# A two-layer block on one core: a new order ahead of a selective scan, the scan's slots in its second half, the tail by halves, and the causal mask of the maxima on VectorE

## The reference

```
mod = silu(c) @ wmod                      # per layer: shift, scale, gate for two branches
# layer 0, branch 1: a selective scan over the tokens, 512 channels, 16 states
h    = layernorm(x) * (1 + scale) + shift
dt_in, B, C = split(h @ x_proj_w.T)       # 16, 16, 16
dt   = softplus(dt_in @ dt_proj_w.T + dt_b)
s_t  = exp(dt_t * A) * s_(t-1) + dt_t * B_t * h_t ;  y_t = sum_n s_t[n] * C_t[n] + D * h_t
x    = x + g(gate) * y                    # g clamps the gate away from zero
# layer 0, branch 2: base linear layer + LoRA experts weighted by softmax routing
w    = top-8 of softmax(h @ router_W.T), summed by expert
x    = x + g(gate) * (h @ base_W.T + b + sum_e w_e (h A_e) B_e)
# layer 1, branch 1: attention, 32 heads of 16, ALiBi, causal
attn = softmax(where(k <= q, q.k / 16 + slope * (k - q), -inf)) ; x = x + g * (attn v @ w_proj + b)
# layer 1, branch 2: gated feed-forward, 1376 wide
```

## Time and profile before

| | |
|---|---|
| median of three runs | 991.18 us (986.23 to 992.69) |
| the profiled execution | 988.8 us, span 987.0 us |
| busy, share of the span | PE 89%, DVE 76%, ACT 45%, POOL 27% |
| mean granted TensorE clock | 0.957 of full |

### The profile page before, as it was taken

How to read it: one execution, slowest core, us unless ns; L and a number is a source line. 1 busy time by engine, 2 the same in 40 slices (tenths; PEclk the granted TensorE clock), 3 DMA queues, 4 the chain that set the end, 5 groups by cost and what they waited for, 6 DMA issues and landing times.

```text
span 987.0 us, 12212 instructions
## 1 busy us (share of the span) xinstructions
PE 877.2 (89%) x4378; PEld 423.7 (43%) x4384; DVE 749.6 (76%) x1191; ACT 439.2 (45%) x822; POOL 264.5 (27%) x213
## 2 busy tenths in 40 slices
PE   3678868887776899989999999999999999999996
PEld 3224424443224544434455555555444444444442
DVE  6579999888899565637887788787524699876776
ACT  1637575645552102110066666666752465533200
POOL 1027789887894300005000000000000144200000
PEclk8769899999997999997999999999999999999998
DMA  9100060300002202451022211220006000000001
GB/s 353 65 1 0 1 255 1 128 0 1 0 0 72 100 0 89 135 181 38 15 69 74 74 37 40 73 75 2 2 1 224 5 0 1 0 1 0 12 33 43
DMA packets 29382, 54.35 MB, mean 55 GB/s; under 512 B 8021, under 2 KB 14805, under 8 KB 28041
## 3 DMA queue, kind: packets, MB, share of 16 engines
q1 hardware_dynamic: 29320, 53.57, 16.2%
HBM read 44.96 MB, written 8.39 MB: 54 GB/s over the span
## 4 chain that ended last, share of the span: by engine, by line
PE 58%; DVE 5%; SPq 3%; issue 3%; ACT 1%; DMA 0%; POOL 0%; DVEq 0%; POOLq 0%
PE ps L1075 15%; PE ps L940 8%; PE ps L922 6%; PE ps L1086 6%; PE ps L904 4%; PE ps L909 3%; PE ps L996 3%; PE ps L976 3%; SPq L302 2%; PE ps L857 2%; PE ps L962 2%; PE ps L925 1%; PE ps L907 1%; PE ps L851 1%; PE ps L725 1%
## 5 line engine op out<-in xcount | busy, mean ns | idle before, releaser
L678 ACT ACTIVATE prob<-ps 128x512 f32<-128x512 f32 x288 | 161.8, 599 | 138.6 <-PE ps L925 105.9
L458 POOL TENSOR_TENSOR hC<-hs,C_sb 128x512 f32<-128x512 f32 x128 | 163.0, 1284 | 70.1 <-DVE hs L1240 59.5
L832 PE MATMUL ps<-hC,identf 128*128 128x512 f32 x256 | 137.1, 644 | 35.6 <-POOL hC L458 33.5
L1354 DVE TENSOR_REDUCE mrow<-ps 128x4 f32<-128x512 f32 x160 | 103.7, 687 | 24.1 <-PE ps L907 15.8
L922 PE MATMUL ps<-stack 123*128 123x512 bf16 (+3 forms) x384 | 113.7, 327 | 0.2
L414 POOL TENSOR_TENSOR rstd<-veps,mhalf 128x4 f32<-128x4 f32 x8 | 8.4, 1052 | 381.4 <-DVE veps L1113 381.4
L612 ACT ACTIVATE ps<-dtT,nA 128x512 f32<-128x512 f32 x128 | 88.3, 691 | 42.2 <-DVE hs L1240 42.0
L1357 DVE TENSOR_REDUCE mrow<-ps 128x1 f32<-128x512 f32 x128 | 82.2, 685 | 25.1 <-PE ps L909 25.1
L832 PEld LDWEIGHTS ps<-hC,identf 128*128 128x128 f32 x256 | 45.3, 197 | 109.5 <-POOL hC L458 90.9
L1218 DVE TENSOR_TENSOR dBx<-uT,ps 128x512 f32<-128x512 f32 x112 | 74.9, 669 | 21.0 <-ACT B_sb L590 14.4
L940 PE MATMUL ps<-prob,V 128*32 128x512 f32 (+3 forms) x768 | 81.6, 498 | 0.7 <-ACT prob L678 0.7
(11 more groups left out here) (192 smaller groups left out, 1328.0 us busy)
## 6 DMA issues: line engine op xcount, KB each, us to landing
stack<-parts_dram SPq DMA_DIRECT2D x192, 64.0 KB
wmod<-in_wmod SPq DMA_DIRECT2D x4, 1536.0 KB, 11.2
parts_dram<-qkp SPq DMA_DIRECT2D x48, 128.0 KB, 1.8
wmod<-in_wmod SPq DMA_DIRECT2D x4, 1024.0 KB, 9.9
wattn<-in_wattn SPq DMA_DIRECT2D x1, 3072.0 KB, 10.3
wg<-in_wg SPq DMA_DIRECT2D x1, 2752.0 KB, 12.2
wu<-in_wu SPq DMA_DIRECT2D x1, 2752.0 KB, 9.5
wd<-in_wd SPq DMA_DIRECT2D x1, 2560.0 KB, 11.5
```

The lines of the kernel that those rows point to most:

```text
L458: pool.tensor_tensor(hC[:, c, :], hs[:, c, :], C_sb[:, m % 2, :], ALU.mult).then_inc(S["hc_done"], 1)
L678: A_(prob[:, u % 4, j, :], ps[:, 3 + F % 3, :], ACT.Exp).then_inc(S["exp_done"], 1)
L832: mm(ps[:, c, :], identf[:], hC[:, c, :], start=False, stop=(s == NS - 1), skip_group_check=True).then_inc(S["sum_done"], 1)
L1354: v.reduce_max(mrow[:, kb, :, i], ps[:, bank, :].rearrange("p (j c) -> p j c", c=P), AX) \
```

## The change

Four places are edited.

- Ahead of the scan: the second half's transposes move behind the first half's split. B and C are split by ScalarE, which copies the negated value in bfloat16, while TensorE adds it to the bank to leave the rest; three such copies per half. The signs of `sel` are turned to match. VectorE takes over the Relu (`arguments`). Half 1's dt_in, split and two of its four `z_out` come ahead of step 0. `dgD` is made earlier.
- Slots: two half rows in place of each full row. In the second half (`m >= 16`) a slot stands ahead of the third sum of a step, once the *next* step's C has been copied out, and ScalarE reads it a step later. Half 1's softplus has four ScalarE operations a step and ends one step earlier on POOL.
- Crossing and tail: `turn(0, c)` and the copies at step 16 are gone. Steps 25 to 28 have slots that make x + gated y of one token tile in bank 4 (identity matmul and four turns), which ScalarE copies to `x_tok`. Behind the scan only half 1 is added. Norm, transposes and router go by halves, with base outputs between them; base_out(4) is made ahead of the LoRA outputs. SP's bias loads wait for `yt`, not `x0`.
- Maxima: the second matmul is gone. Once, TensorE makes the mask in bank 2 and VectorE copies it to `negT` (bfloat16). A diagonal unit is reduced by four `tensor_tensor_reduce`, one per head: add the mask, write the sum to PSUM, and the maximum to `mrow`.

```diff
-            return range(3 * (n - 1), min(3 * n, 7 * DC)) if 1 <= n < NS else range(0)
+            return range(4 * (n - 1), min(4 * n, 7 * DC)) if 1 <= n < NS else range(0)
...
+            SLOTS[1 + i_] = ("cols", 0, 2 + i_ // 2, i_ % 2 * 2)
+        for i_ in range(2):
+            SLOTS[7 + i_] = ("row", 0, 5, i_)
+        for i_, m_ in enumerate((12, 13, 14, 15, 17, 18, 19, 20)):
+            SLOTS[m_] = ("cols", 1, (0, 1, 3, 4)[i_ // 2], i_ % 2 * 2)
+        for i_ in range(4):
+            SLOTS[21 + i_] = ("row", 1, (2, 5)[i_ // 2], i_ % 2)
+            SLOTS[25 + i_] = ("y", None, None, i_)
...
# ScalarE
+            for part in range(3):
+                bc_part(0, part)
+            for c in range(DC - 1):
+                soft(c)
+            ln_out(0, 0, 0, 1, (1,))
+            soft(DC - 1)
...
+            A_(dtin[:], ps[0:RANK, 0, :], ACT.Copy).then_inc(S["xp_in"], 1)
+            bc_part(1, 0)
+            z_out(1)
+            bc_part(1, 1)
+            z_out(2)
+            bc_part(1, 2)
...
-                    if m == NS and c >= 2:
-                        for t in (2 * c - 4, 2 * c - 3):
-                            act.wait_ge(S["yt"], t + 1)
-                            A_(uT[:, t, half(0)], ps[:, t, :], ACT.Copy).then_inc(S["yb"], 1)
...
+                    if c == 2 and m > NS and m - 1 in SLOTS and m - 1 >= NS:
+                        slot_out(m - 1)
# TensorE
+            def bc_rest(h, part):
+                rows = slice(32 * part, 32 * part + 32)
+                pe.wait_ge(S["bc_part"], 2 * h + part + 1)
+                mm(ps[32:64, 0, :], identb[rows, rows], BCs[rows, half(h)], start=False, stop=True, skip_group_check=True) \
+                    .then_inc(S["bc_sub"], 1)
...
+            dt_proj(0, 0)
+            bc_rest(0, 0)
+            dt_proj(0, 1)
+            bc_rest(0, 1)
+            dt_proj(0, 2)
+            dt_proj(0, 3)
+            pe.wait_ge(S["xp_bc"], 1)
+            ln_transpose(0, 1)
             x_proj(1)
...
+                pe.wait_ge(S["c_evac"], m + 1 if m < NS else m + 2)
...
+                    mm(ps[:, C_BANK, :], identf[:], x_tok[:, part, :], start=True, stop=False, skip_group_check=True)
+                    for c in range(DC):
+                        ins = mm(ps[:, C_BANK, c * P:(c + 1) * P], dtT[:, c, tile(part)], dgA[:, c, :], start=False,
+                                 stop=(c == DC - 1), skip_group_check=True)
...
             broadcast(0)
+            pe.wait_ge(S["xp_in"], 2)
+            dt_proj(1, 1)
+            bc_rest(1, 0)
+            dt_proj(1, 2)
+            bc_rest(1, 1)
+            dt_proj(1, 3)
+            pe.wait_ge(S["xp_bc"], 2)
+            dt_proj(1, 0)
...
-                    if c == 0 and m in SLOTS:
-                        modulation(m)
+                    if c == 0 and m in SLOTS and m < NS or c == 2 and m in SLOTS and m >= NS:
+                        slot(m)
...
+            ln_transpose(1, 0)
+            pe.wait_ge(S["in_lf"], 48)
+            router(0)
+            ln_transpose(1, 1)
+            base_out(0)
+            router(1)
+            for t in range(1, 4):
                 base_out(t)
...
+            base_out(4)
             pe.wait_ge(S["hw_evac"], 2)
-            for t in range(4):
+            for t in range(5):
                 lora_out(t)
...
-                        if kb == i:
-                            ins = mm(ps[:, bank, tile(j_)], negm[:], identb[:], start=False, stop=True)
# VectorE
+            def arguments(c):
+                v.wait_ge(S["sp_a"], c + 1)
+                ts(dtT[:, c, half(0)], ps[:, 4 + c, :], dtb[:, c:c + 1], 0.0, ALU.add, ALU.max).then_inc(S["sp_rd"], 1)
...
             ln_var(0)
+            ln_norm(1, 0)
+            for t in range(4, NT):
+                v.wait_ge(S["yt"], t + 1)
+                tt(x_tok[:, t, :], x_tok[:, t, :], ps[:, t, :], ALU.add).then_inc(S["x0"], 1)
...
+                if kb == i:
+                    for j_ in range(GH):
+                        ins = v.tensor_tensor_reduce(ps[:, bank, tile(j_)], ps[:, bank, tile(j_)], negT[:], 1.0, LOW,
+                                                     ALU.add, ALU.max, mrow[:, kb, j_, i:i + 1])
+                    ins.then_inc(S["m_done"], 1)
```

More of the change, by code:

```diff
@@ L542, in _, with bc_part, soft @@
-            for b in range(DC):
-                soft(b)
-            soft_ln(DC - 1)
+            ln_out(0, 0, 0, 1, (0,))
+            def bc_part(h, part):
+                if part:
+                    act.wait_ge(S["bc_sub"], 2 * h + part)
+                else:
+                    act.wait_ge(S["xp_in"], h + 1)
+                A_(BCs[32 * part:32 * part + 32, half(h)], ps[32:64, 0, :], ACT.Copy, scale=-1.0) \
+                    .then_inc(S["xp_bc" if part == 2 else "bc_part"], 1)
+            def soft(c):
+                src = ps[:, 4 + c, :]
+                act.wait_ge(S["dt_mm"], c + 1)
+                A_(sp_log[:, c, :], src, ACT.Abs, bias=dtb[:, c:c + 1]).then_inc(S["sp_a"], 1)
+                act.wait_ge(S["sp_a"], c + 1)
+                link(A_(sp_exp[:, c, :], sp_log[:, c, :], ACT.Exp, scale=-1.0))
+                A_(sp_w[:, c, :], sp_exp[:, c, :], ACT.Copy, bias=1.0).then_inc(S["sp_w"], 1)
+                A_(uT[:, c, half(0)], sp_exp[:, c, :], ACT.Square, scale=SQRT_HALF).then_inc(S["sp_e"], 1)
+                act.wait_ge(S["sp_w"], c + 1)
+                A_(sp_log[:, c, :], sp_w[:, c, :], ACT.Ln).then_inc(S["sp_ln"], 1)
@@ L627, in _ @@
                     decay(m * DC + c)
-                    if m == 0:
-                        z_out(c)
+                    if m == 0 and c < 2:
+                        z_out((3, 0)[c])
                     if m == NS and c < 2:
@@ L748, in x_proj @@
                     pe.wait_ge(S["ln_hT"], 4 * h + kk + 1)
[L749 to L750 removed]
+                    ins = mm(ps[0:64, 0, :], xpw[:, kk, :], hT[:, kk, half(h)], start=(kk == 0), stop=(kk == DC - 1))
                 ins.then_inc(S["xp_mm"], 1)
@@ L769, in modulation @@
                 pe.wait_ge(S["in_w1"] if layer else S["in_wb"], 16 * DC)
-                if c0 is None:
+                if kind == "row":
+                    at_ = j * D + part * D // 2
                     for kk in range(DC):
-                        ins = mm(ps[:, C_BANK, :], sc[:, layer, kk:kk + 1].to_broadcast([P, P]), wmod[:, kk, j * D:(j + 1) * D],
-                                 start=(kk == 0), stop=(kk == DC - 1))
+                        ins = mm(ps[:, C_BANK, 0:D // 2], sc[:, layer, kk:kk + 1].to_broadcast([P, P]),
+                                 wmod[:, kk, at_:at_ + D // 2], start=(kk == 0), stop=(kk == DC - 1))
@@ L835, in _ @@
                     broadcast(NS + 1)
-                    pe.wait_ge(S["dg"], 2 * DC)
-                    for c in range(DC):
-                        turn(0, c)
                     for c in range(DC):
@@ L1256, in _ @@
             for t in range(4):
-                v.wait_ge(S["yb"], t + 1)
-                tt(x_tok[:, t, :], x_tok[:, t, :], uT[:, t, half(0)], ALU.add).then_inc(S["x0"], 1)
-            for t in range(4):
                 v.wait_ge(S["x0"], t + 1)
```

223 lines of the change are left out of this document (97 added, 126 removed).

## The result

| | before | after |
|---|---|---|
| median, four runs each | 991.71 us (986.23 to 992.69) | 947.27 us (946.26 to 947.91) |
| the profiled execution | 988.8 us, span 987.0 | 947.5 us, span 945.7 |
| mean granted TensorE clock | 0.957 | 0.965 |

The ratio is 0.9555 (95% interval 0.9527 to 0.9583). The forecast was 959 us, its range 943 to 975: the direction and the range hold, and 11.4 us more was gained than forecast, 41.3 against 29.9 from execution to execution. The first thing to do is to put the two traces side by side at the same events and to see where the distance between them grows.

A forecast was written before the change was run, and what follows sets the result against it. Bounds: chains of waits ahead of and behind the scan, VectorE in the scan (held up in its second half), TensorE in the attention. Terms summed to -29.9 us from the profiled 988.8, giving 959 us, range 943 to 975.

The forecast's parts named there:

- A: Ahead of the scan: dBx of step 1 comes at 59.1 us against 68.55; -9.0 us (-7 to -11).
- B: First half of the scan: VectorE's gaps at step 7's full-row slot go; -1.5 us (-1.9 to +1).
- C: Crossing between the scan's halves: VectorE's wait of 3.03 us goes; -3.0 us (-2 to -3.3).
- D: Second half of the scan: slots no longer delay the B row, an excess of 11.5 us; -10.3 us (-8 to -11.5).
- The tail: Behind the last scan: working by halves ends LoRA of token tile 6 earlier; -8.6 us (-6 to -9.5).
- F: Attention groups: moving the maxima's mask from TensorE to VectorE gains nothing, group period 31.9 us; taken as +1 us.
- G: QKV stage ahead of the attention: half of VectorE's additional 0.59 us per diagonal unit counts; +1.5 us (-1 to +3).
- T: Attention: spacing of VectorE's masked reductions, taken as 0.30 us between bounds of 0.20 and 0.42.
- The rival with T near 0.20: Attention: back-to-back masked reductions overlap, so TensorE's saving counts; 946 us, chance 0.17.
- The masked reduction as the bound (978, 1012): Attention, two rivals: VectorE bounds at T = 0.42, 978 us, chance 0.16; slower than before at 0.57, 1012 us, 0.04.
- Slots that still delay the B row in the second half: Second half of the scan: two thirds of the slots' excess stays; 967 us, chance 0.10.
- That the new order ahead of the scan gains nothing (968): Ahead of the scan: handovers take what the moves save; 968 us, chance 0.04.

The follow-up runs named there:

- warm: Changed kernel plus five additional matmuls into banks nobody reads, where TensorE idles ahead of x_proj and y_start: 950.71 us, ratio 0.9574.
- slots_first: Changed kernel with the second half's twelve slots back ahead of the next B row: 962.35 us, ratio 0.9696.
- max_alone: Kernel before with only the maxima edit, masked reductions on VectorE in place of TensorE's mask matmuls: 986.23 us against 992.33, ratio 0.993.
- max_undone: Changed kernel with the mask of the maxima back on TensorE, all else as changed: 952.08 us, ratio 0.9594.
- the four versions: Changed kernel with the maxima's mask nowhere, on TensorE, on VectorE (as changed) or on both: QKV stage 113.1, 115.5, 115.6 and 117.9 us.

## Why the prediction was right, and where it was not

**Bounds.** Right: a chain of waits ahead of the scan and in the tail, VectorE in the scan, and TensorE in the attention with VectorE close behind. The experiments undo the maxima, the place of the second half's slots and a piece of the tail's order. No run undoes the order ahead of the scan or the crossing alone: A, B and C rest on the traces.

**The signs.** Held: no VectorE gap in the second half, steps of 6.5 us with slots, the end of the scan (280.07, forecast near 279), the first router matmul at 10.7 us (forecast 11). Missed: dBx of step 1 at 61.56 with a wait of 3.51 us for its B row (forecast 59 and none over 1), gaps of 0.62 and 1.04 us ahead of step 17 (forecast none over 0.5), the group's period of 30.79 us (forecast 31 to 32.5). The wait over 1 us was in my own sum: it has u done at 49.3 and the B row at 59.1, and VectorE's three scans between take some 6. The spacing of 0.25 us lies on the very bound outside of which I had called the prediction failed.

**A, -9.0 forecast, -7.0 measured.** The order did what it was to do: the first scan starts at 53.4 in place of 58.6, and the wait behind the first scans falls from 5.36 to 3.51 us. The step that failed is the durations of TensorE: I timed x_proj from a row of 3.65 us at a granted clock of 1.00, behind sixteen transposes that the change takes away. The same matmuls now take 6.34 us at 0.57 and 6.03 at 0.60; y_start, reckoned at 5.2, takes 6.06 at 0.60. For x_proj of half 1 and y_start `warm` shows that this is the clock; for x_proj of half 0, which delays all behind it by 2.1 us, it is open. The -7.0 lies at the edge of the term's range.

**B, -1.5 forecast, -0.3 measured.** The gaps of the full row are gone, and the two half-row slots (on TensorE from 113.10 and from 120.20, 1.89 us each) leave none. The step that failed is that a column slot costs VectorE nothing. Gaps of 0.62, 0.17 and 0.38 us stand in steps 6 and 7 (101.09 to 109.50), behind the column slots of steps 5 and 6. The first of these took 3.41 us (97.19 to 100.60) at a granted clock of 0.50, where others take 1.84. And the crossing's first dBx waits 1.04 us for B_sb where it had waited next to nothing: the change puts a column slot in step 15, which had none before, ahead of that B row. The gaps now add up to 2.2 us, 0.3 more than before; where the stretch gained 0.6 elsewhere was not traced.

**C, -3.0 forecast, -3.2 measured.** As worked out.

**D, -10.3 forecast, -12.6 measured.** Mechanism right, and `slots_first` shows it. Two sizes were off: I took 0.1 us for each of twelve slots and they cost nothing, and I overlooked a gap of 0.75 us at a step without a slot (288.92 in the trace of before), so the excess was 12.3 rather than 11.5 (14 steps from 192.01 to 295.44, less 14 x 6.51).

**The tail, -8.6 forecast, -10.1 measured.** The order ran as worked out, router at E + 10.7. The transposes took 1.91 us at a granted clock of 1.00 where I had 3.5 and 2.55 (the row of before was at 0.71), and the second router 4.08 at 1.00 where I had 4.87 (0.82); the first took 5.82 at 0.70.

**F, +1 forecast, -6.7 measured; G, +1.5 forecast, -1.5 measured.** This is where 10.7 us lie, of the 11.4 that the forecast missed by. For F `max_alone` and `max_undone` hold it: from the first split to the last the edit takes 6.6 us away in the one and gives 6.7 back in the other. In whole executions it is worth 4 to 6 us (986.23 against 992.33; 952.08 against 947.27). The step that failed is the size of T: 0.30 taken, 0.25 measured. I had bounded it by 0.20 and 0.42 and gone for the nearest single duration, 0.28, plus something for the maximum. A single duration is not a spacing: the row of plain reductions already showed 0.69 long and 0.61 apart. At 0.30 my formula charges VectorE's work with 1.3 us per group, and it costs 0.2 beside TensorE's masks. With T = 0.25 the formula gives 30.6 us per group against 30.79. That TensorE's saving in VectorE's chain counts nothing is neither borne out nor refuted for the changed kernel: 1.19 us counted there, as forecast, but 1.68 without VectorE's masked reductions, and only the sum of the two sides is fixed. The rival with T near 0.20 named 946 us and came nearest in time, without being what happened: T is between the two, F gave 7.7 of the 12 us that it asks of the groups, and the rest of its gain comes from the QKV stage, D and the tail, as luck. The Trainium skill's rule that such an operation is two instructions ("VectorE: DVE Perf Modes", two Vector instructions with no wait between them) is borne out by the pairs in the rows; the estimate of 0.32 us from its cycle table, section on the TRN2 errata, is not, as it adds the accumulator's read where the rows show it beside the next instruction.

G charged VectorE's additional work and put TensorE's saving at nothing. That is the step that failed: in the four versions either mask costs about 2.4 us in this stage, and they change places for nothing (115.5 in `max_undone`, 115.6 after). Why the stage is otherwise shorter (117.2 us before, 116.2 in `max_alone`) is not settled by a run; the difference is no larger than the scatter of 113.8 to 116.5 us between traces with the same code in this stage.

**The rivals.** The masked reduction as the bound (978, 1012) is out at 0.25 us. Slots that still delay the B row in the second half are out: no gap in 98.5 us. That the new order ahead of the scan gains nothing (968) is out at -7.0.

## What to carry to other kernels

When work is moved, take each of TensorE's rows together with the granted clock at which it stands, and ask which clock the new place will have: here 3.65 us at 1.00 became 6.03 at 0.60. The idle time directly ahead does not tell: 3.15 us of it left x_proj at the full clock in one kernel, and behind 2.99 it ran slow in another. Price a short operation of which several come in a row by spacing rather than by duration, and look for a row that has both. Try a change of two sides in all four combinations: that showed that TensorE's masks are worth 1.68 us per group alone and 1.19 beside VectorE's. A wait removed from an engine that is fed by a busy one comes back at the next handover unless the feeder's backlog goes too: here 2.9 of 3.5 us did, while the slots, whose work fitted into TensorE's idle time, gave all of theirs.

## What the runs showed of the hardware

- Eight float32 matmul instructions with 512 columns took 3.65 us at a granted clock of 1.00 (2.4 GHz) and 6.03 us at 0.60, most of them then at the lower level (1.2 GHz). TensorE had idled about 3 us ahead of both, at 1.00 ahead of the fast ones (`warm`) and at 0.50 ahead of the slow ones (the changed kernel).
- A clock at the lower level reached VectorE through a third party: a slot of 16 one-column matmuls took 3.41 us at 0.50 and 1.84 at 1.00, and VectorE waited 0.62 us for the B row behind the slow one.
- The masked reduction on VectorE (128 columns, PSUM to PSUM, with an accumulator) lasts 325 ns and its read 143 ns, yet they come every 0.25 us. Both groups, by line:

```profile
L1399 DVE CUSTOM_DVE_ANT_0 ps<-ps,negT 128x128 f32<-128x128 f32 x256 | 66.3, 325 | 8.8 <-PE ps L960 8.0
L1399 DVE DVE_READ_ACCUMULATOR2_ANT mrow<- 128x1 f32 x256 | 36.6, 143 | 0.0
```

- The same program's profiled executions took 945.7 and 942.3 us of span. The first router alone differs by 1.7 us: 5.82 us at a granted clock of 0.70, and 4.16 at 1.00.
